# Flamingo block on one core: the order of gathers, weight loads and TensorE's work where attention hands over to the experts

## The chip, the cores and the metric

The kernel runs on one core of a Trainium2 chip. The metric is the device time of one execution in microseconds (us), median over runs. Lower is better.

## The reference, cut to what matters

Four sequences of 512 tokens with 256 features. A gated cross attention (16 heads of 16, additive matrix `adj`, padding mask) is followed by a gated top-1 mixture of eight experts:

```python
x = x + tanh(g_xattn) * xattn(layernorm(x), ctx, ctx, adj, mask, ...)   # softmax(Q K^T/4 + adj) V, then Wo
x = x + tanh(g_ffn) * ffn(layernorm(x), ...)

# ffn, per token
probs = softmax(x @ gate_w.T); e = argmax(probs); p = probs[e]
out = (relu(x @ w1[e] + b1[e]) @ w2[e] + b2[e]) * p       # w1: 256x1024, w2: 1024x256, per expert
```

## The kernel before

Each engine has its own program, written out by hand, and they are tied together by semaphores. There are two stages.

**Attention.** For each sequence `b` the loop goes over `TILES` = 64 tiles of scores (128 queries by 512 keys of one head). A tile takes a score matmul (L925), a masked minimum on VectorE (L1560), a shift by the row's extreme on GpSimd (L674, three of four tiles) or ScalarE (L1229), four transposes on TensorE (L935) and an exponential on ScalarE (L1203). Every eight tiles TensorE weighs the values with the exponentials (`weigh`, L947, 16 matmuls in four calls) and ScalarE copies the result to `o_sb` (L1209, for the last group L1287). The tables `USES` and `LAST_USES` say at which tile TensorE does the rest: heads, turns, the output projection, the transposes of normalized rows ("normed", L914), the gate (L890) and the ranking of tokens in their experts ("rank", L875 to L881). `LAST_USES` is for the last sequence. The last two row tiles of the last sequence are finished behind its 64 tiles, in the order of the calls of `last_tail`.

**Experts.** Tokens are put by expert into 23 slots of 128 tokens. The first `EARLY` = 5 slots, s = 0 to 4, can be filled before the last sequence's last tokens are routed; the `LATE` = 18 others, j = 0 to 17, only after them. For a slot, GpSimd gathers the normalized rows (`early_normed`, L653; late `gather_normed`, L741) and the residual rows (`early_x`, L660; late `gather_x`, L747) by indirect DMA; TensorE turns the rows (`early_turn`, L1013; late `turn_rows`, L1089), ScalarE copies them to `xgT` (L1267), TensorE makes the hidden layer in two halves (`early_hidden`, L1025; late L1100), ScalarE applies bias and relu (L1273), TensorE makes the output in two halves of four chunks (`early_y`, L1038; late L1110), VectorE adds bias, weight and residual (early L1669 and L1671, late L1748 and L1754), and GpSimd scatters the rows (early L666, late L753). SyncE loads w1 of the slot's expert, 1 MB, into one of four early buffers (`early_w1`, L481) or two late ones (`load_w1`, L521).

**Between them stands the routing of the last tokens.** The last gate gives logits, VectorE finds each token's expert (L1444 to L1467), TensorE ranks (rank 1), VectorE turns ranks into positions (L1472 to L1483), GpSimd writes token numbers to a table in device memory, `slot_d`, by four indirect DMAs (`to_slots`, L637; two for each of the two halves of the last tokens), and VectorE works out each late slot's expert and base in 20 small steps that end at L1738 and raise `r_eid`. SyncE waits for `r_eid` and for all writes of the table (`r_scat`), loads the token numbers of late slots 0 and 1 (`load_slots`, L513), then w1 of both (L521). GpSimd waits for the token numbers, copies them (L739) and gathers the rows (L741). TensorE waits for `r_eid`, all of w2, and the gathered rows (`f_row0`), turns them, and enters the loop over late experts.

GpSimd, ScalarE, VectorE and SyncE work in strict program order, so what stands behind a waiting instruction waits too. The banks of PSUM: `y_bank(0)` and `y_bank(1)` are banks 5 and 6; `sp_bank` is banks 6 and 7, which the uses take by turns. An early output must find its bank evicted: `early_y` waits on `f_tmp`, which counts evictions of outputs (plus 2 from the start). Before, slot 1 and slot 2 both use bank 5, so slot 2 waits for slot 1's eviction.

The order of TensorE's calls from the end of the 64th tile: turn 0, weigh the last group, hidden 0 first half, heads 0 and 1, turn 1, hidden 0 second half, rank 0, attention turns 0 and 1, hidden 1 first half, out 0 and 1, hidden 1 second half, output 0, turn 2, normed 0 and 1, hidden 2 first half, gate, hidden 2 second half, output 1 first half, rank 1, output 1 second half, then slots 2 to 4, then `turn_rows(0, 0)` and the loop.

## Time and profile before

| | us |
|---|---|
| median of 3 runs | 553.69 |
| the three runs | 556.81, 553.69, 553.6 |
| the profiled execution, own time | 558.52 |
| its span, first to last instruction | 556.8 |
| TensorE matmul busy | 529.3 (95%) |
| VectorE / ScalarE / GpSimd busy | 301.8 / 307.6 / 297.4 |
| mean granted TensorE clock | 0.992 of full |

The page cuts the span into 40 slices of 13.9 us. Times in the rows are from the start of the span. "PE" is TensorE (matmul), "PEld" its weight loads, "DVE" VectorE, "ACT" ScalarE, "POOL" GpSimd, "SPq" the DMA-issuing queue of SyncE. A releaser behind "<-" is what ended an engine's idle time; "issue" means that the profile shows none.

### The profile page before, as it was taken

To read this page: it belongs to the slowest core of one execution; us is meant where nothing else is said; L and a number is where in the kernel's file an instruction comes from. 1 tells how busy PE (TensorE), PEld (TensorE's weight loads), DVE (VectorE), ACT (ScalarE), POOL (GpSimd) and SP (SyncE) were. 2 spreads that over 40 slices of the span, in tenths; PEclk is the share of its full clock that TensorE was granted. 3 is DMA by queue.
4 is the path that set the end of the run, shared out by engine and by line. 5 is a ranking of instruction groups with operands and counts; after the bars stand their busy time and mean duration, and the time that the engine had idled before them with its cause. 6 is when DMAs were issued, how large, how long until landed. Compare 5 with 4: busy or idle time off the path is not lost.

```text
span 556.8 us, 13315 instructions
## 1 busy us (share of the span) xinstructions
PE 529.3 (95%) x4123; PEld 405.7 (73%) x4124; DVE 301.8 (54%) x923; ACT 307.6 (55%) x676; POOL 297.4 (53%) x425
## 2 busy tenths in 40 slices
PE   7999999999999999999999998879898999999996
PEld 5577667667667667666667665549798999999996
DVE  2776577976677976677885877834430110111111
ACT  4366678675678666778675676543232333333331
POOL 6444567665466675468584647451543444444351
PEclk9999999999999999999999999989999999999999
DMA  8633515401315510205520174787345555455660
GB/s 282 207 112 101 183 65 197 138 21 30 123 34 196 149 43 1 78 15 175 182 50 1 35 247 158 247 279 278 68 124 200 200 190 183 180 189 191 195 200 2
DMA packets 51392, 77.23 MB, mean 139 GB/s; under 512 B 9944, under 2 KB 34600, under 8 KB 51208
## 3 DMA queue, kind: packets, MB, share of 16 engines
q1 hardware_dynamic: 46600, 67.72, 36.9%
q0 software_dynamic: 4096, 8.29, 5.2%
q8 instruction: 29, 0.48, 0.4%
q10 hardware_dynamic: 640, 0.52, 0.3%
q14 instruction: 27, 0.22, 0.2%
HBM read 52.76 MB, written 7.89 MB: 109 GB/s over the span
## 4 chain that ended last, share of the span: by engine, by line
PE 53%; DVE 5%; issue 3%; DMA 1%; ACT 1%; POOL 0%; DVEq 0%; ACTq 0%; POOLq 0%
PE bank L1100 12%; PE bank L1110 11%; PE bank L935 8%; PE bank L947 5%; PE bank L925 4%; PE bank L1025 3%; DVE prob L1560 2%; PE bank L1038 2%; PE bank L828 1%; PE bank L909 1%; PE bank L863 1%; DMA parts<-xn_d,eidx 1%; PE bank L1089 1%; PE bank L898 1%; PE bank L890 1%
## 5 line engine op out<-in xcount | busy, mean ns | idle before, releaser
L1560 DVE CUSTOM_DVE_ANT_0 prob<-bank,adjm 128x512 f32<-128x512 f32 x256 | 172.6, 688 | 72.5 <-issue 40.5
L1203 ACT ACTIVATE pt<-bank 128x512 f32<-128x512 f32 x256 | 152.0, 597 | 92.6 <-PE bank L935 85.2
L674 POOL TENSOR_SCALAR prob<-prob,negmax 128x512 f32<-128x512 f32 x192 | 134.2, 702 | 121.6 <-DVE negmax L1560 114.9
L935 PE MATMUL bank<-ident,prob 128*128 128x128 f32 x1024 | 154.7, 274 | 2.2 <-POOL prob L674 1.2
L935 PEld LDWEIGHTS bank<-ident,prob 128*128 128x128 f32 x1024 | 124.4, 141 | 39.8 <-issue 13.4
L1273 ACT ACTIVATE adjm<-bank,colsm 128x128 f32<-128x128 f32 x184 | 52.6, 369 | 105.1 <-PE bank L1100 82.7
L925 PE MATMUL bank<-w2s 128*128 128x512 bf16 x256 | 97.5, 381 | 8.5 <-DVE negmax L1560 6.3
L947 PE MATMUL bank<-pt,vals 128*32 128x256 f32 x1024 | 70.0, 393 | 0.7 <-DVE vals L1360 0.5
L1748 DVE TENSOR_TENSOR cT<-bank,maski 128x256 f32<-128x256 f32 x18 | 7.6, 425 | 115.4 <-PE bank L1110 104.0
L1100 PEld LDWEIGHTS bank<-xT,pt 128*128 128x128 f32 x576 | 67.1, 192 | 1.9 <-ACT xT L1267 1.0
L1100 PE MATMUL bank<-xT,pt 128*128 128x128 f32 x576 | 67.3, 275 | 0.8 <-ACT xT L1267 0.8
L1110 PE MATMUL bank<-w2s,adjm 128*128 x288 | 65.1, 379 | 0.0
L1110 PEld LDWEIGHTS bank<-w2s,adjm 128*128 128x128 f32 x288 | 53.3, 190 | 6.5
L1229 ACT ACTIVATE prob<-prob,negmax 128x512 f32<-128x512 f32 x64 | 46.0, 719 | 11.8 <-DVE negmax L1560 10.4
L925 PEld LDWEIGHTS bank<-w2s 128*128 128x128 bf16 x256 | 25.5, 100 | 31.3 <-issue 15.3
L947 PEld LDWEIGHTS bank<-pt,vals 128*32 128x32 f32 x1024 | 27.2, 111 | 23.8 <-issue 11.3
L739 POOL COPY lidx<-slots 128x1 int32<-128x1 int32 x18 | 3.3, 184 | 48.4 <-DMA slots<-slot_d 48.4
L637 POOL DMA_INDIRECT slot_d<-pair,posi x20 | 21.4, 1068 | 10.6 <-POOL pair L631 3.7
L753 POOL DMA_INDIRECT out_y<-cT,lidx x18 | 18.1, 1005 | 16.0 <-DVE cT L1754 11.1
L741 POOL DMA_INDIRECT rows<-xn_d,lidx x18 | 18.0, 1001 | 14.2 <-POOL lidx L739 14.2
L602 POOL TENSOR_TENSOR adjm<-adjr,maski 128x512 f32<-128x512 f32 x16 | 20.6, 1285 | 1.6 <-ACT maski L1192 1.4
L1560 DVE DVE_READ_ACCUMULATOR2_ANT negmax<- 128x1 f32 x256 | 21.0, 82 | 0.0
(189 smaller groups left out, 612.0 us busy)
## 6 DMA issues: line engine op xcount, KB each, us to landing
pt<-in_L_ffn_w SPq DMA_DIRECT2D x19, 1024.0 KB, 8.9
w2s<-parts SPq DMA_DIRECT2D x96, 128.0 KB
w2s<-in_L_ffn_w SPq DMA_DIRECT2D x8, 1024.0 KB
maski<-in_mask_Bx1xSxS_ik SPq DMA_DIRECT2D x4, 1024.0 KB, 5.5
w2s<-parts SPq DMA_DIRECT2D x56, 64.0 KB, 2.1
xres<-in_x SPq DMA_DIRECT2D x18, 128.0 KB
x_d<-rows SPq DMA_DIRECT2D x18, 128.0 KB
xn_d<-rows SPq DMA_DIRECT2D x18, 128.0 KB
```

Source lines behind the costliest of these rows:

```text
L602: po.tensor_tensor(adjm[:, qt], adjr[:, qt], maski[:, qt].bitcast(F32), ALU.subtract).then_inc(s_adjm, 1)
L637: po.indirect_dma_start(slot_d, bass.IndirectOffsetOnAxis(ap=posi[:, t:t + 1], axis=0), pair[:, t], None, bounds_check=X * TOK - 1, oob_is ...
L674: po.tensor_scalar(prob[:, m], prob[:, m], -1.0, negmax[:, m:m + 1], ALU.mult, ALU.add).then_inc(s_shpool, 1)
L925: pe.matmul(sc_bank[m][:], q, k, start=True, stop=True).then_inc(s_score, 1)
L935: mm = pe.transpose(tr_bank[n % NTB][:, c * P:(c + 1) * P], prob[:, n % TILES % NB, c * P:(c + 1) * P], ident[:])
L947: mm = pe.matmul(pv_bank[32 * j:32 * j + 32, (g % 2) * HALF:(g % 2 + 1) * HALF], vals[:, c, hg * HG + j, :], pt[:, g % 2, c, j, :], start= ...
L1100: mm = pe.matmul(h_bank(u, c), w1s[:, v, k, c * P:(c + 1) * P], xgT[:, u, k], start=k == 0, stop=k == EC - 1)
L1110: mm = pe.matmul(y_bank(u), hT[:, u, c], w2s[:, ds(e, 1), c, :].rearrange("p x e -> p (x e)"), start=c == 0, stop=c == FC - 1)
L1203: act.activation(pt[:, g % 2, :, j, q2 * P:(q2 + 1) * P], tr_bank[c % NTB][:].rearrange("p (c q) -> p c q", c=QT), ACT.Exp).then_inc(s_cac ...
L1229: act.activation(prob[:, m], prob[:, m], ACT.Identity, scale=-1.0, bias=negmax[:, m:m + 1]).then_inc(s_shact, 1)
L1273: act.activation(hT[:, u, c], h_bank(u, c), ACT.Relu, bias=b1c[:, ds(e * FC + c, 1)]).then_inc(f_hT, 1)
L1560: ve.tensor_tensor_reduce(out=prob[:, m % NB], in0=sc_bank[m % NS][:], in1=adjm[:, qt], scale=-1.0, scalar=BIG, op0=ALU.add, op1=ALU.min, ...
```

## The change

Six edits, none of which changes what is computed:

- `LAST_USES`: normed 2, gate 2, normed 3 and gate 3 of the last sequence come one, one, one and two tiles later.
- TensorE: the last group is weighed before turn 0; heads 0 and 1 come before hidden 0; rank 1 comes behind both halves of output 1; `turn_rows(0, 0)` comes between the two halves of output 4, no longer behind them.
- ScalarE: `o_sb` of the last group is copied before `xgT` of slot 0 and the exponential of the first last-token logits.
- Banks: the outputs of early slots 0 to 4 go to banks 5, 5, 7, 6, 5 (before 5, 5, 5, 6, 5), with waits that fit; slot 2 waits for slot 0's eviction and the gate's, slot 3 for slot 0's and rank 1's.
- GpSimd: the gathers of normalized rows for slots 2, 3 and 4 come early, `to_slots` of the first half comes before `tail_rstd`, and `to_slots` of the second half before the residual gather of slot 3 and the scatter of slot 0.
- SyncE: w1 of late slot 0 is loaded as soon as `r_eid` is there, before the wait for `r_scat` and the token numbers; w1 of late slot 1 is loaded only once the rows of late slot 0 have been gathered (`f_row[0]`).

SyncE, from where the late slots are prepared (`pt` holds the late w1, `slots` the token numbers, `in_L_ffn_w` is w1 in device memory; L510 and L518 are the register loads ahead of each DMA). Before:

```order
L510 TENSOR_LOAD base_i [waits t_out0,t_x2T,t_out1,r_scat,r_eid]
...
L513 DMA slots<-slot_d 128x2
...
L513 DMA slots<-slot_d 128x2
L518 TENSOR_LOAD eid
...
L521 DMA pt<-in_L_ffn_w 128x2x1024
L518 TENSOR_LOAD eid
...
L521 DMA pt<-in_L_ffn_w 128x2x1024
```

After the change:

```order
L518 TENSOR_LOAD eid [waits t_out0,t_x2T,t_out1,r_eid]
...
L521 DMA pt<-in_L_ffn_w 128x2x1024
L510 TENSOR_LOAD base_i [waits r_scat]
...
L513 DMA slots<-slot_d 128x2
...
L513 DMA slots<-slot_d 128x2
L518 TENSOR_LOAD eid [waits f_row0]
...
L521 DMA pt<-in_L_ffn_w 128x2x1024
```

One weight load moved ahead of the token numbers, the other behind the arrival of the first gathered rows.

TensorE, from the transposes of tile 64 on (`prob` is a tile of shifted scores, `parts` holds the gathered rows of slot 0, `adjr` its w1, `o_sb` the weighed values). Before:

```order
L935 MATMUL bank<-ident,prob 128x128 [waits cact,shpool]
L935 MATMUL bank<-ident,prob 128x128 x3
L1013 MATMUL bank<-ident,parts 128x128 [waits e_row0,e_eid,masked]
L1013 MATMUL bank<-ident,parts 128x128
L947 MATMUL bank<-pt,vals 32x256 [waits osb,cact]
L947 MATMUL bank<-pt,vals 32x256 x15
L1025 MATMUL bank<-xT,adjr 128x128 [waits f_xgT,e_w10]
L1025 MATMUL bank<-xT,adjr 128x128 x7
L898 MATMUL bank<-ident,o_sb 128x128 [waits md0,osb]
```

After (its lines are numbered one higher here):

```order
L936 MATMUL bank<-ident,prob 128x128 [waits cact,shpool]
L936 MATMUL bank<-ident,prob 128x128 x3
L948 MATMUL bank<-pt,vals 32x256 [waits osb,cact,masked]
L948 MATMUL bank<-pt,vals 32x256 x15
L1014 MATMUL bank<-ident,parts 128x128 [waits e_row0,e_eid]
L1014 MATMUL bank<-ident,parts 128x128
L899 MATMUL bank<-ident,o_sb 128x128 [waits md0,osb]
L899 MATMUL bank<-ident,o_sb 128x128 x3
```

The wait for the gathered rows of slot 0 now stands behind the weighing, and the heads stand before hidden 0.

TensorE, the second half of output 4 and the entry of the late loop. Before:

```order
L1031 TENSOR_LOAD eid
...
L1038 MATMUL bank<-w2s,adjm 128x256
L1089 MATMUL bank<-ident,rows 128x128 [waits f_row0,r_w2,r_eid]
L1089 MATMUL bank<-ident,rows 128x128
L1118 UNCONDITIONAL_BRANCH
...
L1100 MATMUL bank<-xT,pt 128x128 [waits f_xgT]
```

After:

```order
L1089 MATMUL bank<-ident,rows 128x128 [waits f_row0]
L1089 MATMUL bank<-ident,rows 128x128
L1038 TENSOR_LOAD eid
...
L1048 MATMUL bank<-w2s,adjm 128x256
L1129 UNCONDITIONAL_BRANCH [waits r_w2,r_eid]
...
L1112 MATMUL bank<-xT,pt 128x128 [waits f_xgT]
```

The transposes of late slot 0 now have four output matmuls and a register load behind them, ahead of the loop.

```diff
--- before.py
+++ after.py
@@ -105,8 +105,8 @@
     LAST_USES = sorted([(10, "values", 0), (11, "values", 1), (13, "heads", 0), (14, "heads", 1), (16, "turn", 0),
                         (18, "turn", 1), (20, "out", 0), (22, "out", 1), (27, "normed", 0), (29, "normed", 1),
                         (31, "gate", (0, 1)), (39, "rank", 0), (45, "heads", 2), (46, "heads", 3), (48, "turn", 2),
-                        (50, "turn", 3), (52, "out", 2), (54, "out", 3), (59, "normed", 2), (61, "gate", (2,)),
-                        (62, "normed", 3), (64, "gate", (3,))], key=lambda use: use[0])
+                        (50, "turn", 3), (52, "out", 2), (54, "out", 3), (60, "normed", 2), (62, "gate", (2,)),
+                        (63, "normed", 3), (66, "gate", (3,))], key=lambda use: use[0])
     LAST_TAIL = [("heads", 0), ("heads", 1), ("rank", 0), ("turn", 0), ("turn", 1), ("out", 0), ("out", 1),
                  ("normed", 0), ("normed", 1), ("gate", (0, 1)), ("rank", 1)]
     RANKED = ((0, 2), (2, 4))
@@ -321,7 +321,7 @@
             return bank[5 + u][:, 0:E]
 
         def early_y_bank(s):
-            return y_bank(0 if s == 1 else s % 2)
+            return (y_bank(0), y_bank(0), sp_bank[1][:, 0:E], y_bank(1), y_bank(0))[s]
 
         block = st.enter_context(nc.Block(no_gpsimd_drain=True))
 
@@ -521,11 +521,12 @@
                 sp.dma_start(w1s[:, v], w1_v[ds(e, 1)].rearrange("x p k f -> p (x k) f")).then_inc(f_w1[v], 16)
 
             sp.wait_ge(r_eid, 1)
+            load_w1(0, 0)
             sp.wait_ge(r_scat, (B + 1) * (16 * QT))
             for v in range(2):
                 load_slots(v, v)
-            for v in range(2):
-                load_w1(v, v)
+            sp.wait_ge(f_row[0], 16)
+            load_w1(1, 1)
             with sp.Fori(0, LATE // 2 - 1) as i:
                 for v in range(2):
                     load_slots(i * 2 + (v + 2), v, i * 2 + v + 1)
@@ -712,24 +713,24 @@
                     step(b, n)
             for n in range(LAG, LAG + TILES):
                 step(B - 1, n, True)
+            early_normed(2)
             early_x(0)
-            early_normed(2)
+            wait_apart(po, s_osb, B * GROUPS + 2)
+            early_normed(EROWS)
             early_x(1)
             early_x(2)
-            for k in range(2):
-                tail_rstd(B, k)
+            early_normed(EROWS + 1)
             pairs(B, B)
             for t in range(*RANKED[0]):
                 to_slots(t)
-            for s in range(EROWS, EARLY):
-                early_normed(s)
-            early_x(EROWS)
-            early_scatter(0)
+            for k in range(2):
+                tail_rstd(B, k)
             pairs(B, B + 1)
             for t in range(*RANKED[1]):
                 to_slots(t)
+            early_x(EROWS)
+            early_scatter(0)
             early_x(EROWS + 1)
-
             for s in range(1, 3):
                 early_scatter(s)
 
@@ -1026,11 +1027,20 @@
                                        start=k == 0, stop=k == EC - 1)
                     mm.then_inc(f_h, 1)
 
+            def tail_free(use):
+
+                i = LAST_TAIL.index(use) + LAST_SHIFT
+                assert i % 2 == int(use[0] == "gate")
+                return free(B, i) + 1
+
             def early_y(s, half):
                 u = s % 2
                 e = pe.value_load(eid[0:1, s:s + 1], min_val=0, max_val=X - 1)
                 if half == 0:
-                    pe.wait_ge(f_tmp, s + (2 if s in (1, 2) else 1))
+                    pe.wait_ge(f_tmp, (1, 3, 3, 3, 4)[s])
+                    if s in (2, 3):
+
+                        pe.wait_ge(s_md[s % 2 ^ 1], tail_free(("gate", (0, 1)) if s == 2 else ("rank", 1)))
                     pe.wait_ge(r_w2, 16 * X)
                 for c in range(half * FC // 2, (half + 1) * FC // 2):
                     pe.wait_ge(f_hT, s * FC + c + 1)
@@ -1045,14 +1055,14 @@
             for n in range(LAG, TILES + LT):
                 step(B - 1, n, LAST_USES, True)
             pe.wait_ge(s_masked, B * TILES)
+            for c in range(QT):
+                weigh(B - 1, GROUPS - 1, c)
             pe.wait_ge(e_eid, 1)
             early_turn(0)
-            for c in range(QT):
-                weigh(B - 1, GROUPS - 1, c)
-            early_hidden(0, 0)
             pe.wait_ge(s_osb, B * GROUPS + 2)
             last_tail("heads", 0)
             last_tail("heads", 1)
+            early_hidden(0, 0)
             early_turn(1)
             early_hidden(0, 1)
             last_tail("rank", 0)
@@ -1071,24 +1081,26 @@
             last_tail("gate", (0, 1))
             early_hidden(2, 1)
             early_y(1, 0)
+            early_y(1, 1)
             last_tail("rank", 1)
-            early_y(1, 1)
-            for s in range(2, EARLY):
-                if s + 1 < EARLY:
-                    early_turn(s + 1)
-                for half in range(2):
-                    early_y(s, half)
-                if s + 1 < EARLY:
-                    for half in range(2):
-                        early_hidden(s + 1, half)
-
-
             def turn_rows(i, v):
                 pe.wait_ge(f_row[v], i * 16 + 16)
                 for k in range(EC):
                     mm = pe.transpose(xg_bank((v + EARLY) % 2)[:, k * P:(k + 1) * P], rows[:, v, E + k * P:E + (k + 1) * P],
                                       ident[:])
                 mm.then_inc(f_xt, 1)
+
+            for s in range(2, EARLY):
+                if s + 1 < EARLY:
+                    early_turn(s + 1)
+                for half in range(2):
+                    if s + 1 == EARLY and half == 1:
+                        turn_rows(0, 0)
+                    early_y(s, half)
+                if s + 1 < EARLY:
+                    for half in range(2):
+                        early_hidden(s + 1, half)
+
 
             def expert(j, i, v, last=False):
                 u = (v + EARLY) % 2
@@ -1114,7 +1126,6 @@
 
             pe.wait_ge(r_eid, 1)
             pe.wait_ge(r_w2, 16 * X)
-            turn_rows(0, 0)
             with pe.Fori(0, LATE // 2 - 1) as i:
                 for v in range(2):
                     expert(i * 2 + v, i, v)
@@ -1281,11 +1292,11 @@
 
             for n in range(LAG, TILES + LE):
                 step(B - 1, n, LAST_USES, True)
-            turned_rows(0, 0)
-            route_exp(B, *RANKED[0])
             act.wait_ge(s_pv, B * GROUPS)
             act.activation(o_sb[:, heads_of(GROUPS - 1), (GROUPS - 1) // NG],
                            pv_bank[:, (GROUPS - 1) % 2 * HALF:((GROUPS - 1) % 2 + 1) * HALF], ACT.Copy).then_inc(s_osb, 1)
+            turned_rows(0, 0)
+            route_exp(B, *RANKED[0])
             act.wait_ge(e_eid, 1)
             e = expert_of(0)
             hidden(0, 0, e, 0)
```

## Rows read from the trace of the kernel before

**Rows 1.** The page's head.

```profile
span 556.8 us, 13315 instructions
```

**Rows 2.** Chain that ended last, late stage: start, us, what.

```profile
429.31 3.57 PE bank L1100 x32
...
545.23 3.57 PE bank L1100 x32
```

**Rows 3.** Timeline: start, us, engine, line, operation [idle before <-releaser], end of attention.

```profile
359.25 0.44 PE L914 MATMUL bank<-ident,rows 128*128 128x128 f32 x2 [0.89 <-DVE rows L1419]
...
368.40 0.66 PE L935 MATMUL bank<-ident,prob 128*128 128x128 f32 x4 [0.51 <-POOL prob L674]
370.94 0.66 PE L1013 MATMUL bank<-ident,parts 128*128 128x128 f32 x2 [1.88 <-DMA parts<-xn_d,eidx]
371.53 3.64 PE L947 MATMUL bank<-pt,vals 128*32 128x256 f32 x32
...
369.10 0.60 ACT L1203 ACTIVATE pt<-bank 128x512 f32<-128x512 f32 x1 [0.37 <-PE bank L935]
```

**Rows 4.** Busy time by stretch: PE, PEld, DVE, ACT, POOL; granted clock, DMA share, GB/s.

```profile
350.00:360.00 10.00, 7.89 (x72) 5.29 (x65) 8.83 (x30) 5.66 (x10) 4.47 (x8) 1.00 0.83 289
...
370.00:371.00 1.00, 0.06 (x1) 0.09 (x2) 0.00 (x0) 0.00 (x0) 0.76 (x1) 0.66 0.55 164
...
377.00:378.00 1.00, 1.00 (x10) 1.00 (x10) 0.00 (x0) 0.00 (x0) 0.00 (x0) 0.93 1.01 341
```

**Rows 5.** Timeline of TensorE from rank 1 to the first late expert.

```profile
398.26 0.20 PE L875 MATMUL bank<-onehot,ones 128*128 128x8 bf16 x2 [0.25 <-DVE onehot L1460]
...
399.19 1.99 PE L1038 MATMUL bank<-w2s,adjm 128*128 x8 [0.68 <-issue]
...
401.89 3.72 PE L1038 MATMUL bank<-w2s,adjm 128*128 x16 [0.49 <-DVE cT L1669]
...
416.26 3.62 PE L1038 MATMUL bank<-w2s,adjm 128*128 x16
420.63 0.41 PE L1089 MATMUL bank<-ident,rows 128*128 128x128 f32 x2 [0.75 <-issue]
421.80 3.83 PE L1100 MATMUL bank<-xT,pt 128*128 128x128 f32 x32 [0.76 <-ACT xT L1267]
```

**Rows 6.** Timeline of VectorE: output 1, and the routing's last step.

```profile
401.32 0.42 DVE L1669 TENSOR_TENSOR cT<-bank,maski 128x256 f32<-128x256 f32 x1 [1.19 <-PE bank L1038]
...
406.47 0.23 DVE L1738 TENSOR_SCALAR base_i<-bf,least 128x19 int32<-128x19 f32 x1
```

**Rows 7.** Timeline of SyncE's DMA issues, late slots.

```profile
409.94 1.84 SPq L513 DMA_DIRECT2D slots<-slot_d  x2
412.56 1.55 SPq L521 DMA_DIRECT2D pt<-in_L_ffn_w  x2
421.25 0.37 SPq L513 DMA_DIRECT2D slots<-slot_d  x1
425.81 0.38 SPq L521 DMA_DIRECT2D pt<-in_L_ffn_w  x1
427.16 0.34 SPq L513 DMA_DIRECT2D slots<-slot_d  x1
```

**Rows 8.** Timeline of GpSimd: last write of the table, copies of token numbers, a gather.

```profile
402.44 1.07 POOL L637 DMA_INDIRECT slot_d<-pair,posi  x1 [0.30 <-DVE cT L1671]
...
413.18 1.01 POOL L741 DMA_INDIRECT rows<-xn_d,lidx  x1 [0.83 <-POOL lidx L739]
...
423.41 0.18 POOL L739 COPY lidx<-slots 128x1 int32<-128x1 int32 x1 [2.85 <-DMA slots<-slot_d]
...
432.08 0.18 POOL L739 COPY lidx<-slots 128x1 int32<-128x1 int32 x1 [5.39 <-DMA slots<-slot_d]
```

**Rows 9.** DMA issues from 405 to 420 us: count, median us to landing.

```profile
out_y<-cT,eidx POOLq DMA_INDIRECT x3, 3.0
```

**Rows 10.** The same on the page, whole span.

```profile
out_y<-cT,lidx POOLq DMA_INDIRECT x18, 3.7
```

## The prediction

> **What bounds the kernel now.** I read the chain that ended last first. Its late part is one pattern: 32 hidden matmuls, two turns, 16 output matmuls, on TensorE alone, with no gap. Sixteen experts lie between its rows at 429.31 and 545.23 [rows 2], so one takes 115.92 / 16 = 7.25 us, and 18 late experts take the last quarter of the span. The change doesn't touch them. What it can win lies ahead of the first late hidden matmul, at 421.80 [rows 5]: every microsecond by which that moves moves the end.
>
> The timeline of TensorE shows where that engine stands still between the 64th tile and 421.80. The last transposes start at 368.40 and end at 369.06; then TensorE waits 1.88 us for the gathered rows of slot 0 [rows 3]. Later it waits 0.25 for the one-hot of rank 1, 0.68 behind rank 1, 0.49 for the eviction of output 1, 0.75 before the turn of late slot 0, and 0.76 for ScalarE's copy of that turn [rows 5]. Last, the table of stretches: the granted clock is 0.66 in the microsecond from 370 and 0.93 in that from 377 [rows 4], so TensorE fell to its lower level, 1.2 GHz, at about 370.3, inside the 1.88 us of idleness, and came back to 2.4 GHz at about 377.1.
>
> **Weighing first (TensorE, ScalarE).** Weighing needs only ScalarE's last exponential, which starts at 369.10 and takes 0.60 [rows 3]. So it can start at 369.75 where the turn of slot 0 started at 370.94: 1.2 us won. The rows of slot 0 landed at about 370.8, so they are there when the turn comes behind the weighing. The heads now follow at once and need ScalarE's copy of the weighed group; a turn of about 0.3 lies between, the copy takes about as long as the exponential at most, so TensorE waits about 0.3: cost 0.3. The copies for slot 0 and the exponential of the logits go behind it on ScalarE, and their users (hidden 0, rank 0) come more than 1 us later.
>
> **The clock.** From 370.94 to 377.1 TensorE was busy at half clock: 6.2 us did the work of 3.1. In the changed kernel the longest standstill here is 0.7 us (369.06 to 369.75), beside two of 0.51 (one of them in [rows 3]). A standstill of 0.89 at 359.25 [rows 3] lies in a stretch whose clock is 1.00 [rows 4]. So I take it that the clock doesn't fall here: 3.1 us won. Bounds: 0 if it falls all the same, 3.1 if not. Together the front wins 1.2 + 3.1 - 0.3 = 4.0 us at output 0.
>
> **Rank 1 behind output 1; other banks.** TensorE no longer stands 0.25 before rank 1, and the 0.68 behind it goes: that gap is the register load of the second half, which stood behind a blocked instruction. Slot 2 has its own bank 7, so the 0.49 goes. Won: 1.42. Bounds: 0.9 (if the evictions of the gate's and the rank's banks, now waited for, take up the 0.49) to 1.42. Output 4's first half then ends 5.4 us earlier than before: 416.26 + 1.75 - 5.4 = 412.6.
>
> **LAST_USES.** The 0.89 for normed 2 goes. It is worth nothing: the last tiles wait for GpSimd (the 0.51 before 368.40 [rows 3] is for its shift), and GpSimd for an index load that the change leaves alone. If that cover were gone it would be worth 0.9 at most; bounds 0 to 0.9.
>
> **GpSimd's order.** Three gathers of normalized rows go ahead. Two of them now wait for turns 0 and 1 of TensorE; what is queued behind them is residual gathers, whose users are outputs over 10 us later, and `to_slots`, which is due only after rank 0, behind turn 1. The second pair of table writes starts 1.0 us after the positions as before, nothing ahead of it. I cost it at nothing; bounds -0.3 to +0.3, one issue gap.
>
> **The routing chain, which decides.** Before, the turn of late slot 0 waited for its gathered rows: both other waits were long over, and 0.75 us of standstill precede it [rows 5]. The chain: rank 1 at 398.26 [rows 5], output 1 held up VectorE until 401.32, the last table step ends at 406.70 [rows 6]; the last table write starts at 402.44 [rows 8]; SyncE issues token numbers at 409.94 and two weight loads from 412.56 [rows 7]; the gather starts at 413.18 [rows 8]; the rows are turned at 420.63 [rows 5]: 7.4 us from gather to rows, beside 2 MB of weights.
>
> After: output 1's second half is ahead of rank 1. The first half ends at 398.01 - 4.0 = 394.0, the second 1.75 later, so rank 1 comes at 395.75, 2.5 earlier. VectorE stood 1.19 before output 1's eviction, until TensorE was done [rows 6]; now output 1 is ready first, and only the register load is left of it: between 0 and 1.19 won, I take 0.4, since such a load behind rank 1 cost TensorE 0.68. `r_eid` comes at 406.70 - 2.9 = 403.8. SyncE needs about 1.1 from a release to its issue, as between its two loads of token numbers (the pair spans 1.84, an issue 0.37 [rows 7]; 1.84 - 0.37 = 1.47 holds one of them, so 1.1). Weights 0 are issued at 404.9. The table's writes: before, start at 402.44, SyncE's issue at 409.94, less 1.1, so all landed at about 408.85, 6.4 us later. Now they start 2.5 earlier and land at 406.3, so the token numbers are issued at 407.4.
>
> How long do these take behind a weight load? Alone, issued at 421.25 and copied by GpSimd at 423.41: 2.15. Behind one, issued at 427.16, copied at 432.08: 4.9, which is 6.25 after the weight load's issue at 425.81 [rows 7, 8]. So they land between 407.4 + 2.15 = 409.5 and 404.9 + 6.25 = 411.1; I take the middle, 410.3. The Trainium skill ("DMA: Bandwidth & Descriptors", "Queues, rings and completion order") says that each DMA engine takes the descriptors of one ring in order, and SyncE's transfers share their rings. It speaks against putting the weights first, and the trace agrees (4.9 against 2.15); by it alone the later end, 411.1, would hold and the time be 0.8 us longer.
>
> From token numbers to a gather's start: 0.18 for the copy and 0.83 behind it, 1.0 [rows 8]. The gather now has no weight load beside it: indirect transfers that were seen to land took 3.0 [rows 9] and 3.7 [rows 10]; it may still take the 7.4 of before. I take 3.35, since the load that made it 7.4 is held back. The rows are there at 410.3 + 1.0 + 3.35 = 414.65 (413.5 to 419.5).
>
> TensorE arrives at 412.6 and stands for 2.1 us. Then turn, register load and output matmuls: from rank 1 at 398.26 to the next output matmul at 399.19 was 0.93 in the same situation, and a half output is 1.75. The first late hidden matmul starts at 414.65 + 0.1 + 0.93 + 1.75 = 417.4, against 421.80: 4.4 us won. ScalarE's copy hides behind the half output.
>
> **Weights 1 held back.** Issued about 1.1 after 414.65, so 415.8; there about 6 us later, 421.8 (before, both within 8.5 of 412.56); needed at 417.4 + 7.25 = 424.7. Cover of 2.9 us; if a load took 9 us it would cost nothing yet.
>
> **The sum.** Against the profiled execution, 558.52 with a span of 556.8 [rows 1]: 4.4 less, 554.1. But its median is 553.69, 4.8 below. The three runs are 553.6, 553.69 and 556.81: one stands 3.2 above the others, the size of the 3.1 us of the fallen clock. I read this as two executions where the clock didn't fall at 370 and one where it did, as in the profile. Then 3.1 of the 4.4 are not in the median: 4.4 - 3.1 = 1.3, and 553.69 - 1.3 = 552.4. **Forecast: 552.4 us.**
>
> **Rivals.**
> - *The fall is in every run of before* (chance 0.2). The 4.4 count in full: 553.69 - 4.4 = 549.3. For it: the profile shows the fall. Against: the spread of 3.2 has then no reason.
> - *The rows come before TensorE does* (0.12). If the token numbers aren't held up and the gather takes 2 us or less, the late stage starts at 412.6 + 0.44 + 1.75 = 414.8, 7.0 earlier; less the 3.1, 3.9: 549.8. Against: no indirect transfer in the rows landed in under 3.0.
> - *The new standstill makes the clock fall* (0.23), the slower side. A standstill of 1.88 did so at 370. The turn before output 4's second half stands for 2.1, and 0.5 follows. If the clock falls there, up to 3.1 us are lost as before: 552.4 + 3.1 = 555.5, 0.3% above before. It decides from about 1.5 us of standstill on; the 0.89 didn't do it. Against: a short turn and the output split it, and 1.2 us already separate the two known cases.
> - *The gather takes 7.4 whatever is beside it* (0.05): rows at 418.7, first late hidden at 421.5; 0.3 won, less 3.1: 556.5.
>
> The forecast has 0.4. The first two rivals together, 546.7, are the corner in which it is faster by over 1%.
>
> **Numbers.** About 1% (5.5 us) is what a measurement of this kernel tells from no change. Faster by more than that, below 548.2: 0.09, from the corner and from half the span of the first rival's bounds. Slower, above 559.2: 0.03, both losses together. Same: 0.88. Range 549.0 to 555.8: it holds the forecast, the first three rivals and their bounds of 0.3.
>
> **What would show it.** Right: TensorE's weighing follows the last transposes after 0.7 us and its matmuls take about half of 3.64; granted clock 1.00 from 370 to 380; rank 1 with no gap before or behind it; no wait for output 1's eviction; `r_eid` about 2.9 earlier; the turn of late slot 0 behind a standstill of about 2 us; the first late hidden near 417.4; 7.25 per late expert. Wrong: a clock below 1.00 near 414; a standstill before expert 6 (weights 1 late); token numbers more than 6.3 after weights 0; a late turn with no standstill.

## The result, and the profile after

The changed kernel takes **558.71 us**, the median of four runs (558.0 to 560.46). The kernel before, timed beside it, takes 553.79 (553.6 to 556.81). The ratio is 1.007, with an interval of 1.0037 to 1.0104: slower by 0.7%, within the 1% that I had called no change, but 6.3 us above the forecast and 2.9 above the end of the range.

The page's head answers to [rows 1]; this execution took 558.0 us:

```profile
span 556.2 us, 13269 instructions
```

The timeline of the same execution, first TensorE, then VectorE, SyncE and GpSimd (start, us, engine, line, operation, idle before and its releaser); it answers to [rows 3] and [rows 5 to 8]:

```profile
367.79 0.66 PE L936 MATMUL bank<-ident,prob 128*128 128x128 f32 x4 [0.16 <-POOL prob L675]
369.17 1.93 PE L948 MATMUL bank<-pt,vals 128*32 128x256 f32 x32 [0.73 <-issue]
...
395.07 0.20 PE L876 MATMUL bank<-onehot,ones 128*128 128x8 bf16 x2
...
395.43 3.62 PE L1048 MATMUL bank<-w2s,adjm 128*128 x16
...
409.70 1.89 PE L1048 MATMUL bank<-w2s,adjm 128*128 x8
416.62 0.69 PE L1089 MATMUL bank<-ident,rows 128*128 128x128 f32 x2 [5.03 <-DMA rows<-xn_d,lidx]
417.39 3.77 PE L1048 MATMUL bank<-w2s,adjm 128*128 x8
420.96 4.15 PE L1112 MATMUL bank<-xT,pt 128*128 128x128 f32 x32
...
402.06 0.29 DVE L1749 TENSOR_SCALAR base_i<-bf,least 128x19 int32<-128x19 f32 x1
...
403.10 0.40 SPq L521 DMA_DIRECT2D pt<-in_L_ffn_w  x1
406.92 1.50 SPq L513 DMA_DIRECT2D slots<-slot_d  x2
417.31 0.40 SPq L521 DMA_DIRECT2D pt<-in_L_ffn_w  x1
...
398.64 0.97 POOL L638 DMA_INDIRECT slot_d<-pair,posi  x1 [0.30 <-issue]
...
412.75 0.19 POOL L740 COPY lidx<-slots 128x1 int32<-128x1 int32 x1 [6.52 <-DMA slots<-slot_d]
413.76 1.02 POOL L742 DMA_INDIRECT rows<-xn_d,lidx  x1 [0.83 <-POOL lidx L740]
```

The front does what was forecast: weighing 0.73 us behind the transposes, in 1.93 instead of 3.64; rank 1 without a gap before or behind it; no wait for output 1's eviction. But everything won on TensorE comes back in one piece, the standstill of 5.03 us ahead of the late turn. The chain of waits names what TensorE stands for (start, us, what):

```profile
413.76 2.82 DMA rows<-xn_d,lidx
416.62 0.69 PE bank L1089 x2
417.39 3.77 PE bank L1048 x8
```

Half an output takes 3.77 us there, against 1.89 for the other half at 409.70. The stretches say why (busy time of PE, PEld, DVE, ACT, POOL, granted clock, DMA share, GB/s), to be held against [rows 4]:

```profile
370.00:380.00 10.00, 9.60 (x95) 8.49 (x85) 3.71 (x18) 4.59 (x17) 5.28 (x8) 1.00 0.84 285
...
412.00:414.00 2.00, 0.00 (x0) 0.00 (x0) 0.00 (x0) 0.00 (x0) 0.42 (x2) 1.00 0.00 0
414.00:416.00 2.00, 0.00 (x0) 0.00 (x0) 0.00 (x0) 0.00 (x0) 1.17 (x3) 0.75 0.20 57
416.00:418.00 2.00, 1.30 (x4) 0.81 (x5) 0.00 (x0) 0.38 (x1) 1.70 (x2) 0.50 0.17 41
418.00:420.00 2.00, 2.00 (x6) 1.64 (x5) 0.00 (x0) 0.00 (x0) 1.39 (x3) 0.50 0.85 211
420.00:422.00 2.00, 2.00 (x9) 1.73 (x9) 0.65 (x2) 0.00 (x0) 0.59 (x1) 0.55 1.03 406
422.00:424.00 2.00, 2.00 (x20) 2.00 (x20) 0.26 (x1) 0.54 (x3) 0.18 (x1) 1.00 0.38 138
```

The clock doesn't fall at 370 any more; it falls at 415 instead, to 1.2 GHz, and is back by 422. The first late hidden matmul is at 420.96, 0.84 ahead of [rows 5]. So the two profiles alone would tell "a little faster", where the timed runs say slower. That contradiction is what the experiments had to settle.

### The profile page after: what moved, and what is told of

Read it like the earlier page. It is cut to its first block, busy times and chain, and to the rows that moved or that the text cites. A ratio compares the mean times of both kernels' runs of the same rounds, so it can differ in the third digit from the quotient of the medians.

```text
span 556.2 us, 13269 instructions
## 1 busy us (share of the span) xinstructions
PE 522.7 (94%) x4075; PEld 406.4 (73%) x4124; DVE 301.5 (54%) x923; ACT 307.1 (55%) x676; POOL 296.5 (53%) x425
## 4 chain that ended last, share of the span: by engine, by line
PE 47%; DVE 5%; DMA 4%; issue 3%; SPq 1%; POOL 1%; ACT 0%; DVEq 0%; another core or an unknown queue 0%; POOLq 0%; ACTq 0%
PE bank L1112 12%; PE bank L1122 11%; PE bank L936 7%; PE bank L948 4%; PE bank L926 3%; DVE prob L1571 3%; PE bank L1026 2%; PE bank L1048 2%; DMA slots<-slot_d 2%; PE bank L829 1%; PE bank L910 1%; DMA slot_d<-pair,posi 1%; PE bank L864 1%; PE bank L1089 1%; PE bank L899 1%
## 5 line engine op out<-in xcount | busy, mean ns | idle before, releaser
L926 PE MATMUL bank<-w2s 128*128 128x512 bf16 x208 | 79.2, 381 | 7.2 <-DVE negmax L1571 5.4
L948 PE MATMUL bank<-pt,vals 128*32 128x256 f32 x1024 | 68.3, 385 | 1.5 <-issue 0.7
```

The lines of the kernel that those rows point to most:

```text
L926: pe.matmul(sc_bank[m][:], q, k, start=True, stop=True).then_inc(s_score, 1)
L948: mm = pe.matmul(pv_bank[32 * j:32 * j + 32, (g % 2) * HALF:(g % 2 + 1) * HALF], vals[:, c, hg * HG + j, :], pt[:, g % 2, c, j, :], start= ...
```

## The experiments

Each ratio is against the kernel before, run on the same chip beside it; a 95% interval stands behind each. That kernel's median differed between these sets of runs (554.15 to 558.84), so only ratios are compared. The changed kernel itself was timed only in the set of the result; where a variant of it is held against its 1.007, the two ratios come from different sets.

### First: the SyncE part and the late turn

**The kernel before, again** (no edit).

> The kernel before, unchanged, run again to see its spread. Its timed runs were 553.6 to 556.81, its profiled one 558.52. Theory 'clock at 370': the spread is the fall of TensorE's clock near 370 us, present in some executions; then runs near 553.7 have a mean granted clock near 1.00 (about 0.998) and those near 556.8 one near 0.992. Rival 'waits on transfers': the clock is alike (0.992) in all and the spread comes from when gathered rows land; then spans differ by 3 us or more at the same clock.

0.9981 [0.9934, 1.0028]. Its profile (span 559.2) has a standstill of 3.05 ahead of the late turn, where [rows 5] has 0.75, and its first 32 late hidden matmuls take 5.46 us instead of 3.83. So the kernel before has executions of its own in which the rows of late slot 0 are late and the clock falls. Of its ten runs the two shortest have mean granted clocks of 0.999 and 0.997 and the two longest 0.991 and 0.989, but one in the middle, 3.5 us longer in span than the shortest, has 1.000: the clock goes with a part of the spread only. What makes up the rest, the times alone don't say.

**SyncE's order undone.**

```
-            load_w1(0, 0)
             sp.wait_ge(r_scat, (B + 1) * (16 * QT))
             for v in range(2):
                 load_slots(v, v)
-            sp.wait_ge(f_row[0], 16)
-            load_w1(1, 1)
+            for v in range(2):
+                load_w1(v, v)
```

> The changed kernel with SyncE's part undone (token numbers of both late slots first, then both weight loads), all else as changed. Theory 'weights first cause the standstill': token numbers land about 2.2 us after their issue instead of 5.7, the gather starts near 409.5 and, now beside two weight loads again, lands 6 to 7.4 us later, near 416.5; the standstill in front of the late turn stays at 4 to 5 us and the clock falls there too; time 557 to 559, no better than the changed kernel by more than 1. Rival 'the whole loss is SyncE's order': the standstill is under 2 us, the clock stays at its upper level, time 550 to 553.

1.0081 [1.0046, 1.0116]: nothing comes back that this interval can tell. Its profile has the standstill of 4.22 that was expected.

**SyncE's order alone, on the kernel before** (the same lines the other way).

> The kernel before with SyncE's part of the change alone. Theory 'weights first cause the standstill': weights 0 go out near 407.8, token numbers are issued near 409.9 as before and land 4.9 to 5.7 later instead of 2.2, the gather then starts near 416.5 and lands in 2.8 us, 419.3; the late turn is 1 us earlier at most to 1 us later than in before (420.6); time within 1 us of before, 552.7 to 555. Rival 'SyncE's part alone loses 5': time 557 to 559.

1.0001 [0.9957, 1.0045]. SyncE's order alone costs or wins nothing beyond the interval, which leaves about 0.4% either way.

**The late turn back behind output 4**, first with SyncE's order undone too, then alone.

```
-                    if s + 1 == EARLY and half == 1:
-                        turn_rows(0, 0)
                     early_y(s, half)
...
             pe.wait_ge(r_w2, 16 * X)
+            turn_rows(0, 0)
```

> The changed kernel with SyncE's part undone and the turn of late slot 0 put back behind output 4; the front (weighing first, banks, rank 1, GpSimd's order) stays. Theory 'the late start is held by the routing chain': TensorE reaches the late turn at about 413.5 with rows near 416.5, so 3 us of standstill; first late hidden near 418 to 418.5 and the clock falls for part of it; time 553 to 556. Rival 'the front gain reaches the end': first late hidden near 416.5, time 549 to 551.

1.0084 [1.0046, 1.0123]. Its profile has a standstill of 3.48 ahead of the late turn, and the first late hidden takes 5.99.

> The changed kernel with the turn of late slot 0 put back behind the whole of output 4; SyncE's part stays as changed. Theory 'the turn in the middle of output 4 keeps half an output behind the late rows': from the rows' landing to the first late hidden 1.2 us instead of 4.3, so 3 us faster than the changed kernel if the clock falls as much, and the standstill shrinks from 5 to 3.3 us. Rival 'the clock falls in the late hidden layer instead': the first late hidden takes 5.5 to 6 us instead of 4.2, so only 1.0 to 1.5 us are won.

1.0062 [1.002, 1.0104]. No gain shows from the turn's place either. The profile of the second shows something else, on ScalarE and then on TensorE, which waits for it:

```profile
405.48 1.14 ACT L1283 ACTIVATE adjm<-bank,colsm 128x128 f32<-128x128 f32 x4 [4.95 <-PE bank L1026]
412.25 1.14 ACT L1283 ACTIVATE adjm<-bank,colsm 128x128 f32<-128x128 f32 x4 [5.63 <-remote]
...
412.77 1.99 PE L1048 MATMUL bank<-w2s,adjm 128*128 x8 [3.70 <-ACT adjm L1283]
```

The matmuls for that eviction ended at about 407.1, and ScalarE takes it up 5 us later; the view gives as releaser "remote", which is none of the five engines. I come back to it below. This profile is also the fastest of the ten runs (559.27, median 562.8), and the output matmuls behind its standstill of 3.70 take 1.99: the clock did not fall here. A stretch in which TensorE stood still, and the one behind:

```profile
411.00:412.00 1.00, 0.00 (x0) 0.00 (x0) 0.00 (x0) 0.00 (x0) 0.00 (x0) 1.00 0.66 115
412.00:413.00 1.00, 0.23 (x1) 0.23 (x2) 0.00 (x0) 0.75 (x3) 0.00 (x0) 1.00 0.88 344
```

### The clock by itself

Matmuls whose result nobody reads stand ahead of the late turn, behind a wait for output 3's eviction, so that TensorE isn't idle there: 36 in the changed kernel, 28 in the variant with SyncE and turn undone, 16 in the kernel before.

```
+                        pe.wait_ge(f_tmp, EARLY + 1)
+                        keep_busy(36, bank[6])
                         turn_rows(0, 0)
```

> The changed kernel with 36 matmuls of 256 columns, about 4 us of work whose result nobody reads, in front of the wait for the rows of late slot 0, so that TensorE is busy while it waits; the expert outputs are as before. Theory 'the standstill makes the clock fall': clock 1.00 from 410 to 425, the second half of output 4 takes 1.9 instead of 3.8 us and the first late hidden 3.7 to 3.8 instead of 4.2, so the kernel gains 2.0 to 3.0 us on the changed one (0.4 to 0.5%). Rival 'the clock costs nothing, only the late rows do': no gain, within 0.7 us of the changed kernel, or slower because the extra matmuls end after the rows have landed.

1.0117 [1.003, 1.0204].

> The kernel with the changed front alone (SyncE's part undone, turn behind output 4) and 28 matmuls of 256 columns, about 3 us, ahead of the wait for late rows. Without them it was 0.8% slower than before and had 3.5 us of standstill and a first late hidden of 6.0 us instead of 3.8. Theory 'clock': the first late hidden takes 3.7 to 3.8, time 2.2 us or more below the one without the matmuls, so at most 0.5% slower than before. Rival 'something else in the front is slower': it stays 0.7 to 0.9% slower than before at a clock of 1.00.

1.0107 [1.0008, 1.0205].

> The kernel before with 16 such matmuls, about 1.7 us, between output 4 and the late turn. Theory 'before also loses clock there in some executions': the spread narrows and the median falls by 0.5 to 1.5 us against before. Rival 'before never stands long enough': same time, within 0.3 us.

1.0027 [0.9982, 1.0072]. The granted clock is 1.00 from the late turn on in all three profiles, and none is faster. These runs don't price the clock. The 36 matmuls take 4.09 us, from 420.79, and in that profile output 3 waited 3.77 for ScalarE as above (the clock did fall there). The gather had started at 417.61; if it took the 2.82 of the changed kernel, the rows were there before the matmuls had begun. The runs show only that a fixed filler brought no gain, two of them with four runs each and wide intervals. That the clock makes up 2 to 3 us of the loss was my theory; nothing here bore it out or refuted it, and I looked for what else puts the rows late.

### The remaining parts, one at a time on the kernel before

**GpSimd's order alone**, as in the diff above.

> The kernel before with the changed order of GpSimd's transfers alone (the three gathers of normalized rows ahead, the factors of the last tiles' normalization behind them, the first residual gather of the late tail and the first scatter behind the second table writes). Theory G: this order is where the time went (residual gathers and scatters meet the table writes and ScalarE's and VectorE's instruction loads); then the ratio to the kernel before is 1.006 to 1.008 here, and 1.000 in the other three. Theory S: the time goes in what changed ScalarE's stream; then 1.000 +- 0.003 here, since ScalarE's instructions are those of before.

**LAST_USES alone.**

> The kernel before with LAST_USES of the changed kernel alone (normed 2 and 3 and the gates of tiles 2 and 3 one or two steps later). Theory S1: these steps move ScalarE's and VectorE's instructions against the points at which their next instructions are loaded; then 1.003 to 1.008. Rival, what the prediction said: they wait for something else anyway, 1.000 +- 0.002, with the standstill of 0.89 us before normed 2 gone.

**Weighing first alone**, TensorE's and ScalarE's order.

> The kernel before with weighing first on TensorE, and ScalarE's copy of the last weighed group ahead of the copies for slot 0. Theory S2: ScalarE's other order moves the point at which it waits for instructions to a dearer place; 1.004 to 1.008, and the profile shows a wait of 2 us or more on ScalarE between 380 and 415 us that ends hidden 1 or 3 late. Rival, the prediction: weighing 1.2 us earlier and no fallen clock near 370 us, which the routing chain passes on to the end: 0.995 to 0.998. A third: as the routing chain's end is set by VectorE, 1.000.

**Rank 1 behind output 1, and the banks.**

> The kernel before with rank 1 behind the second half of output 1 and the other banks for outputs 2 and 3. Theory R: rank 1 comes 1.75 - 0.25 = 1.5 us later than before, the table writes and the late turn with it; 1.003, and the gap between outputs 1 and 2 is gone but comes back before the late turn. Rival, the prediction: only the gaps of 0.25, 0.68 and 0.49 go and the chain loses 1.5 less 0.4: within 1.000 to 1.002.

GpSimd 1.0056 [1.0035, 1.0078]; LAST_USES 1.0003 [0.9984, 1.0023]; weighing 1.0018 [1.0, 1.0036]; rank 1 with banks 1.0041 [1.0013, 1.0069].

Weighing first, the largest term of the prediction, wins nothing by itself; the 0.995 to 0.998 that it stood for lies outside the interval. In its profile weighing takes 1.93, but ScalarE then copies the weighed group late, with the releaser "remote" (374.37, idle for 4.53), TensorE stands for it, and the heads behind take 1.90 instead of 1.04:

```profile
374.81 1.90 PE L898 MATMUL bank<-ident,o_sb 128*128 128x128 f32 x8 [2.57 <-ACT o_sb L1285]
```

Rank 1's part, with the banks, costs 0.4% by itself. Its profile, TensorE's timeline:

```profile
419.69 0.41 PE L1098 MATMUL bank<-ident,rows 128*128 128x128 f32 x2 [2.99 <-DMA rows<-xn_d,lidx]
420.77 6.71 PE L1109 MATMUL bank<-xT,pt 128*128 128x128 f32 x32 [0.68 <-issue]
```

The same pattern: a standstill for the rows, then 32 matmuls in 6.71 us instead of 3.83. (This execution has a fallen clock at weighing, 2.85, and waits for "remote" as well, so its 6.71 isn't the price of the part.) GpSimd's part is stranger; in its profile VectorE, behind TensorE's rank 0, and ScalarE, at a relu of the hidden layer, wait for "remote" again, and TensorE with them:

```profile
380.58 1.14 ACT L1274 ACTIVATE adjm<-bank,colsm 128x128 f32<-128x128 f32 x4 [3.59 <-remote]
...
380.54 0.17 DVE L1473 TENSOR_TENSOR place<-bank,region 128x16 f32<-128x16 f32 x1 [2.98 <-remote]
...
381.06 0.41 PE L905 MATMUL bank<-ident,attn 128*128 128x128 f32 x2 [2.39 <-DVE region L1476]
```

### Halves of GpSimd's order, and parts taken back out

**Only the three gathers ahead; only the residual gather and scatter behind the second table writes, and `tail_rstd` behind the first.**

> The kernel before with the early half of GpSimd's change alone: the three gathers of normalized rows ahead (five transfers in a row from slot 2's residual rows to slot 4's normalized ones, then the rank's writes). Theory G1: this train falls beside rank 0, where VectorE and ScalarE wait 3.0 and 3.6 us and TensorE 2.4 in the profile of GpSimd's whole change; 1.004 to 1.006. Rival G2: the late half costs, and this gives 1.000 +- 0.002.

1.0002 [0.9988, 1.0016].

> The kernel before with the late half of GpSimd's change alone: slot 3's residual gather and the first scatter behind the second table writes, and the factors of the tails' normalization behind the first ones. Theory G2: seven transfers in a row then stand beside the second table writes and SyncE's loads, which hold up the rows of late slot 0; 1.004 to 1.006. Rival G1: 1.000 +- 0.002.

1.0017 [1.0, 1.0034]. The halves don't make the whole's 0.56%. Why the whole costs more stays open; neither half's profile has the waits for "remote".

These two profiles gave what I had lacked: TensorE's instructions as before, and no fallen clock at weighing, no standstill at the late turn, no wait for "remote". I call this the undisturbed chain. It is that of variants (spans 552.4 and 552.6); no profile of the unchanged kernel without such a disturbance was taken. The second one's timeline, TensorE, then SyncE and GpSimd:

```profile
369.89 0.66 PE L935 MATMUL bank<-ident,prob 128*128 128x128 f32 x4 [0.51 <-POOL prob L674]
372.06 0.41 PE L1013 MATMUL bank<-ident,parts 128*128 128x128 f32 x2 [1.51 <-DMA parts<-xn_d,eidx]
372.40 1.93 PE L947 MATMUL bank<-pt,vals 128*32 128x256 f32 x32
...
396.04 0.19 PE L875 MATMUL bank<-onehot,ones 128*128 128x8 bf16 x2
...
398.83 3.72 PE L1038 MATMUL bank<-w2s,adjm 128*128 x16 [0.49 <-DVE cT L1669]
...
413.20 3.62 PE L1038 MATMUL bank<-w2s,adjm 128*128 x16
416.66 0.38 PE L1089 MATMUL bank<-ident,rows 128*128 128x128 f32 x2
417.58 3.84 PE L1100 MATMUL bank<-xT,pt 128*128 128x128 f32 x32 [0.54 <-ACT xT L1267]
...
407.77 1.84 SPq L513 DMA_DIRECT2D slots<-slot_d  x2
410.39 1.55 SPq L521 DMA_DIRECT2D pt<-in_L_ffn_w  x2
...
409.66 0.19 POOL L739 COPY lidx<-slots 128x1 int32<-128x1 int32 x1 [2.35 <-DMA slots<-slot_d]
410.68 1.10 POOL L741 DMA_INDIRECT rows<-xn_d,lidx  x1 [0.83 <-POOL lidx L739]
```

TensorE doesn't stand at all ahead of the late turn: the rows are there when it comes. The standstill for slot 0 is 1.51, and weighing takes 1.93, so the clock didn't fall. From the end of the last transposes (370.55) rank 1 comes 25.49 later and the first late hidden 47.03 later. In the profile on which I predicted these are 29.20 and 52.74.

**GpSimd's order taken out of the changed kernel; then GpSimd's order, rank 1's place and the banks; then rank 1's place alone** (the lines of the last):

```
-            early_y(1, 1)
             last_tail("rank", 1)
+            early_y(1, 1)
```

> The changed kernel with GpSimd's order of the kernel before; all else stays changed. Theory G (GpSimd's order costs 0.56% by itself: its long train of transfers falls where VectorE's and ScalarE's next instructions are wanted, ahead of rank 0): it takes the cost along, 1.001 to 1.003 times the kernel before, where the changed kernel stands at 1.007. Rival: the parts don't add up, and any changed order of the streams costs as much: 1.006 to 1.008 still.

1.0085 [1.006, 1.0109]: nothing back. That GpSimd's order alone carries the cost (theory G) falls.

> The changed kernel with GpSimd's order, and rank 1 and the banks of outputs 2 and 3, as before. What is left: SyncE's order, LAST_USES, weighing first, the late turn inside output 4. If the two parts that cost most alone (0.56% and 0.41%) carry all of it: 0.998 to 1.001. Rival (parts don't add up): 1.005 or more.

1.0019 [0.9998, 1.004]: nearly all back.

> The changed kernel with rank 1 ahead of output 1's second half, as before; the other banks, GpSimd's, SyncE's and the other orders stay changed. Theory R (the routing chain sets the start of the late experts, and rank 1 behind 1.75 us of output makes it late): rank 1 24.9 us after the last transposes instead of 26.6, standstill ahead of the late turn 2 to 3 us instead of 5.0, no fallen clock there; 1.001 to 1.003 times the kernel before. Rival B (the banks of outputs 2 and 3 with their waits cost): 1.006 to 1.008 still. Rival G (rank and GpSimd's order each cost and only both together give it back): 1.004 to 1.006.

1.0059 [1.0037, 1.008]. This lies where rival G put it, and outside the 1.001 to 1.003 of theory R; rival B's 1.006 to 1.008 isn't excluded by this interval, but in the next experiment the same banks come without a cost. Neither GpSimd's order nor rank 1's place, taken out alone, gives the time back; with the banks both together do. The two profiles beside each other, first rank 1's place alone back, then all three back, TensorE at the late turn:

```profile
417.04 0.44 PE L1089 MATMUL bank<-ident,rows 128*128 128x128 f32 x2 [3.63 <-DMA rows<-xn_d,lidx]
417.80 3.58 PE L1048 MATMUL bank<-w2s,adjm 128*128 x8 [0.33 <-issue]
421.18 3.87 PE L1112 MATMUL bank<-xT,pt 128*128 128x128 f32 x32
```

```profile
414.97 0.44 PE L1079 MATMUL bank<-ident,rows 128*128 128x128 f32 x2 [1.82 <-DMA rows<-xn_d,lidx]
415.74 1.99 PE L1038 MATMUL bank<-w2s,adjm 128*128 x8 [0.33 <-issue]
417.56 3.73 PE L1102 MATMUL bank<-xT,pt 128*128 128x128 f32 x32
```

Behind 3.63 us of standstill the half output takes 3.58, behind 1.82 it takes 1.99. So the price isn't linear: a standstill that grows costs its growth, and where the clock falls, here 1.6 us more. Whether it falls isn't settled by the length alone, since the 3.70 above left it at 1.00.

**The rest of TensorE's changes without rank 1's place**: weighing first, banks and LAST_USES on the kernel before. This was the candidate to beat both.

> The kernel before with weighing first, the other banks for outputs 2 and 3 and LAST_USES of the changed kernel; rank 1, SyncE, GpSimd and the late turn as before. Theory R: these only shorten TensorE's part, which sets the late start in executions of the kernel before where nothing disturbs it (20.6 us from rank 1 to a late turn with no standstill): 0.49 for the bank and 0.6 for the weighing, 0.997 to 0.999, faster than both kernels. Rival: the rows of late slot 0 come no earlier, and a standstill takes the place of both: 1.000 to 1.002.

1.0006 [0.9983, 1.003]: the same as before. The rival is what came. TensorE's timeline and the stretches behind:

```profile
417.67 0.41 PE L1098 MATMUL bank<-ident,rows 128*128 128x128 f32 x2 [2.11 <-DMA rows<-xn_d,lidx]
418.80 5.40 PE L1109 MATMUL bank<-xT,pt 128*128 128x128 f32 x32 [0.73 <-ACT xT L1276]
```

```profile
418.00:420.00 2.00, 1.27 (x6) 1.20 (x6) 0.00 (x0) 0.38 (x1) 0.00 (x0) 0.67 0.37 117
420.00:422.00 2.00, 2.00 (x12) 2.00 (x11) 0.00 (x0) 0.00 (x0) 0.97 (x2) 0.50 0.00 0
```

TensorE was ready earlier, stood for the rows and lost its clock. This profile is the slowest of the twelve runs, which lie between 550.9 and 557.28, where 16 of before lie between 552.27 and 556.16: some executions win and some lose.

### The profiles side by side

Microseconds from the end of the last transposes, each read from TensorE's timeline; that end and the span, both from the start of the span, stand in the last two columns. "Through" is where the output matmuls ahead of the late turn end.

| profile | rank 1 | through | late turn | standstill | first late hidden | transposes end | span |
|---|---|---|---|---|---|---|---|
| before, undisturbed (late half of GpSimd) | 25.49 | 46.3 | 46.11 | 0 | 47.03 | 370.55 | 552.6 |
| before, as predicted on | 29.20 | 50.8 | 51.57 | 0.75 | 52.74 | 369.06 | 556.8 |
| weighing, banks, LAST_USES | 24.89 | 44.9 | 47.03 | 2.11 | 48.16 | 370.64 | 555.5 |
| GpSimd, rank, banks back | 24.90 | 44.0 | 45.77 | 1.82 | 48.36 | 369.20 | 552.4 |
| rank 1's place back | 25.45 | 43.7 | 47.38 | 3.63 | 51.52 | 369.66 | 556.2 |
| GpSimd back | 26.63 | 43.2 | 47.85 | 4.68 | 52.01 | 369.12 | 556.0 |
| changed kernel | 26.62 | 43.1 | 48.17 | 5.03 | 52.51 | 368.45 | 556.2 |

From the third row down TensorE is through 1.4 to 3.1 us earlier than in the first, and none of it reaches the first late hidden: the late turn follows the rows, and the hidden matmuls come 1.1 to 5.5 later than undisturbed, latest in those whose standstill is long. Of the kernels timed, the upper four stand within 0.2% of before, the lower three 0.6 to 0.85% above. (The medians don't repeat the order among those three; their intervals overlap.)

## Why the prediction was wrong

The miss is 6.3 us. Counted from the last transposes, 2.6 of it is the base, 2.5 the rows' arrival and 1.7 what lies between the late turn and the first late hidden matmul, the clock above all. Against that, the last transposes end 2.1 earlier in the changed kernel's profile than in the undisturbed one, for which no run gives a reason; the medians lie 1.3 further apart than these two profiles, and 0.2 lies behind: together the 6.3, but for rounding. TensorE's own side came out: it was through 43.1 behind the transposes, where I had forecast 43.5.

**The base was an unusual execution.** That is the step that failed first. I corrected the profile for one thing, the fallen clock, by 3.1 us. Against an undisturbed execution it is 52.74 - 47.03 = 5.7 us long up to the first late hidden matmul: 3.7 ahead of rank 1 and 2.0 behind it. In the 3.7 are the clock and a wait of VectorE with the releaser "remote": it takes up the last gate's logits at 396.06, and TensorE's matmuls for them began at 393.44 and took 0.96, so they were ready 1.7 us before; the standstills of 0.25 and 0.68 at rank 1 [rows 5] are absent undisturbed too, so that of the 1.42 that I had rank 1's place and the banks win 0.93 wasn't there to win. My own forecast of the late start, 417.4, is 48.3 from the end of the transposes. Held against 47.03 it says slower by 1.3, not faster by 1.3: these are the 2.6.

**Rank 1's place.** I had TensorE win 4.0 at output 0 and set the 1.75 of output 1's second half against it. Undisturbed, the front's own gain at rank 1 is 25.49 - 24.90 = 0.6, and rank 1's place costs 26.62 - 24.90 = 1.7 of the routing chain. Net 1.1 later, not 2.5 earlier. The time of rank 1 itself I had right (26.7 forecast, 26.62 measured); what it stood against was wrong.

**Token numbers behind weights.** This term I had mis-sized. From the end of the transposes, `base_i` was 0.8 earlier than forecast, SyncE's issue of the token numbers 0.1 later, but they were copied at 412.75, 5.83 behind their issue and 9.65 behind that of the weights (forecast: 2.9 and 5.4, and 6.25 as the late end). Undisturbed and issued ahead of weights, the copy comes 1.89 behind the issue. The Trainium skill's sentence on the rings' order ("DMA: Bandwidth & Descriptors", "Queues, rings and completion order") spoke for the later end, and the trace went past that end. The gather then took 2.82, 0.5 less than forecast. Counted from rank 1 the copy comes 17.68 behind it (412.75 - 395.07), undisturbed 13.62 (409.66 - 396.04). In the changed kernel with SyncE's order undone it comes 14.59 behind, so of the 4.1 us between them 3.1 are SyncE's order. The gather gives back: beside two weight loads it took 5.2 from its start to the turn in that profile and 6.2 in the one of rank 1's part alone, here 2.9. Both together leave the turn about 0.8 later than with SyncE's order undone (48.17 against 47.37 behind the transposes), too little for the timed runs to tell. So my sign of being wrong, token numbers more than 6.3 after weights 0, came true.

**The clock.** At 370 the forecast holds: no fall, 1.93 for weighing. At the late turn the rival with 0.23 came in. I had priced it by 3.1 at most and put its point at about 1.5 us of standstill. Measured here: 3.77 - 1.89 = 1.9 in the half output and 4.15 - 3.73 = 0.4 in the first hidden, 2.3 together; no fall behind 1.82, a fall behind 2.11 in another kernel, and no fall behind 3.70 in a third. So no length of standstill seen here says from where on the clock falls.

**The turn inside output 4.** ScalarE's copy hides, as forecast, but the half output stands behind the rows: 4.34 us from turn to first late hidden, against 0.92 undisturbed. I counted 1.75 of it in the path and didn't see that the order before has those 1.75 done by then. Since a_turn_back's run is no faster than the others, this alone isn't the cost; it moves the standstill from one side of the half output to the other.

Sum, against the undisturbed chain: 1.13 for rank 1, 0.93 between rank 1 and the late turn, 3.42 between turn and hidden (1.9 clock, the rest the half output), 0.2 behind: 5.7 us from the end of the transposes. The spans differ by 3.6, since the changed kernel's transposes end 2.1 earlier; the medians differ by 4.9, and the ratio says 3.9. That rank 1's place with the banks has a cost is measured (1.0041 alone), and so is that it and GpSimd's order together hold nearly all (1.0019 without both). That the way is "rows later than TensorE, then the clock" is read from the profiles of the table, one execution each, and is not shown by an experiment: no run took the rows' lateness away with all else kept. Another way stands untested beside it: each variant has its own order of instructions, and with it its own waits for "remote", of which the timed executions may hold more than the profiled ones.

LAST_USES (1.0003), the second table write's gap and the weights held back (landed in time; the second late expert has no standstill) went as forecast. Weighing first did on TensorE what was forecast, but of the 4.0 us nothing reached the time when it stood alone (1.0018).

## What to carry to other kernels

Before a sum is made, ask whether the profiled execution is one of those that the median stands for: here two undisturbed profiles, at 552.5 of span, told more than the one at 556.8. Where an engine and a chain of small transfers arrive together at a handover, making the engine earlier won nothing here, and whatever it is given to do ahead of the chain's own small step (here 1.75 us ahead of rank 1) is paid at the handover. And a standstill there can have a second price, the clock behind it: 1.6 to 2.9 us where it fell.

## What the runs showed of the hardware that I had not expected

- **The clock's second price, and that it isn't certain.** Standstills of TensorE and the first 32 late hidden matmuls behind them: 0 and 1.24 us, 3.84 and 3.83; 2.11, 5.40; 2.99, 6.71; 3.05, 5.46; 3.48, 5.99. The granted clock falls to 0.50, 1.2 GHz, in the stretches shown. But no length of a single standstill parts the cases. At the turn of slot 0, 1.51 and 1.65 (the profile with 16 filler matmuls) left weighing at 1.93, 1.57 (LAST_USES alone) was followed by 3.28 and 1.88 [rows 3] by 3.64; and of two waits for ScalarE's "remote", one of 3.70 was followed by half an output in 1.99 and one of 3.59 by the same in 3.78.
- **ScalarE and VectorE take up ready work late.** In 9 of 20 profiles one of them stands 2.3 to 5.7 us with the releaser "remote", between 370 and 413 us, at work that was ready 1.7 to 5 us before. The place goes with the order of the instructions: it ends at 393.5 to 396.4 (VectorE) and 396.6 to 399.5 (ScalarE) in the kernel before and in four made from it, at 374.4 too in the one with weighing first; at 380.5 with GpSimd's order; at 380.3 to 382.1 and 411.5 to 413.1 in three variants of the changed kernel. The same kernel has them in one execution and not in another. I suspected loads of instructions; the records of such loads don't end where these waits end, so the cause stays open.
- **A load of 1 KB behind one of 1 MB.** From its issue to its use 4.1 to 6.2 us in the seven profiles in which weights 0 had been issued ahead (5.83 in the changed kernel), 1.9 to 3.5 in the thirteen others.
- **An indirect gather beside weight loads.** From its start to the waiting turn 2.8 to 2.9 us in five profiles with no weight load issued just ahead, 5.2 to 6.9 in five with 2 MB of them.
